# Four of a layer's seven products taken as three fp32r passes, on high and low parts made by GpSimd

## The chip, the cores and the metric

The kernel runs on one core of one Trainium2 chip. The metric is the device time of one execution, in microseconds, lower is better. The engines are named as the profile names them: PE is TensorE (PEld its weight loads), DVE is VectorE, ACT is ScalarE, POOL or Pool is GpSimd, SP is SyncE, which issues most DMAs.

## What is computed

The reference is a recommender tower: 39 embeddings of 16 numbers are gathered for each of 512 samples, pass through three layers of a compressed interaction network, and go with 16 context features through a small dense net. Cut to what matters:

```python
e = jnp.stack([tbl_f[ids[:, f]] for f in range(39)], axis=1)         # 512 x 39 x 16
def _cin_layer(X0, Xi, W, b):                                         # H = 128 outputs
    Wr = W.reshape(H, X0.shape[1], Xi.shape[1])
    return jnp.einsum('hjk,bjd,bkd->bhd', Wr, X0, Xi) + b[None, :, None]
Xi, res = e, []
for W, b in ((W0, b0), (W1, b1), (W2, b2)):
    Xi = _cin_layer(e, Xi, W, b)
    res.append(Xi.sum(axis=2))
h = jnp.concatenate([jnp.concatenate(res, axis=1), dense_ctx], axis=1)
h = relu(h @ W_top1 + b_top1); h = relu(h @ W_top2 + b_top2); y = h @ W_top3
```

Everything is float32.

## The kernel before, in words

**Tiling.** The 512 samples are 16 groups of 32. A group is 4 tiles of 128 columns (8 samples by 16 dims), so a group's operands are 512 columns wide. The kernel is a software pipeline with one period for each group. Every engine has a program of its own, written out by hand, and the engines meet at semaphores. From period 1 on, PE, DVE, Pool and SP run it in hardware loops of two periods.

**Second layer.** In period g, PE takes 10 banks for each of the 4 tiles (`layer1_bank`, L979 to L997). A bank is 512 columns (the tenth 384), in three passes at reduced input precision (fp32r): high by high, low weights by high, high weights by low. ACT multiplies seven of the ten banks by the field values (L634), DVE the other three (L795, L800), DVE adds all of them up (L816) and folds the sums (L822). The banks live in rings, 4 for ACT's and 2 for DVE's, and PE may refill one only when DVE has added its contents.

**First layer.** It is done one group ahead: during period g, PE makes the first layer of group g+1 in seven products c = 0 to 6 (`layer0`, L950), each of `w0t[:, c]` by `pairs[:, c]`, 117 rows (78 for c = 6) by 512 columns in plain float32, accumulated in the bank `p0`. A slot (t, m) is the place behind bank m of tile t. `LAYER0_SLOTS` puts the seven products at (0,4), (0,9), (1,4), (1,8), (2,4), (2,9) and (3,4). The last one releases `l0_done`; ACT then takes the high part of `p0` (L617) and DVE the low part (L771), which are the next period's operands.

**Pairs.** `pairs[:, c]` is the product of the field values `x0r` with a shifted copy of them. ACT copies `x0r` out of PSUM at slot (2,7) (L577, `copy_fields`, which also waits until all pairs of the group before are made), SP writes it to DRAM (L331) and reads it back shifted (L344): the first half (c = 0 to 3) at once, the second half after `l0_done`. Pool multiplies in place (`pair_chunk`, L479): c = 0 to 3 of group g+2 at the end of period g, c = 4 to 6 of group g+1 in tile 0 of period g.

**Pool's other work** stands in the same program order (L488 to L505): in each tile the block-diagonal operand of `gram_product` (`spread`, L474, which waits for a gram product of PE), and the ten gathers of the embeddings of group g+3 (L427), two in tile 0, four in tile 1, four in tile 2. ACT takes the gathered rows at slot (0,2) of the next period (`dims_outside`, L584).

## Time and profile before

| | us |
|---|---|
| median of 3 runs | 681.0 (680.91 to 682.17) |
| the profiled execution, its own time | 682.09 |
| its span, first to last instruction | 680.3 |
| PE busy | 646.9 (95%) |
| DVE busy | 572.9 (84%) |
| ACT busy | 561.3 (83%) |
| POOL busy | 359.6 (53%) |
| mean granted clock of PE | 0.995 |

A timeline row gives the start, the duration, the engine, the line of the kernel, the operation with output and inputs, and in brackets how long the engine stood idle before it and what ended that. Matmuls overlap, so what one takes is the distance to the next start, not its duration. Of Pool's rows, too, distances are used.

### The profile page before, as it was taken

The numbers are of one execution on the slowest core, as the hardware profiler recorded it, in microseconds if no ns is written. First come the engines' busy times: TensorE is split into PE (matmuls) and PEld (weight loads), VectorE is DVE, ScalarE is ACT, GpSimd is POOL, SyncE is SP. The second block draws the span as 40 slices with busy tenths as digits, with TensorE's granted clock in tenths as the row PEclk, the third lists the DMA queues.
The fourth block names the chain that finished last, engine by engine and source line by source line (L and its number), as shares of the span: only waits on it lengthen the run. The fifth ranks groups of instructions, "written<-read, shape, count | busy, mean of one in ns | idle before, by whom it ended". The sixth has DMA issues, their size and how long they took to land.

```text
span 680.3 us, 11318 instructions
## 1 busy us (share of the span) xinstructions
PE 646.9 (95%) x2662; PEld 483.9 (71%) x2662; DVE 572.9 (84%) x894; ACT 561.3 (83%) x1941; POOL 359.6 (53%) x394
## 2 busy tenths in 40 slices
PE   2789989999999999999999999999999999989898
PEld 2656767777777777777777777777777777767584
DVE  2548878989898998989898989898989899999870
ACT  2339879989898989988888989898989888899762
POOL 7554884664747474838384756557474323142700
PEclk9898999999999999999999999999999999999999
DMA  8215631405051414141322314050504040200000
GB/s 285 22 16 117 157 48 25 97 13 109 10 112 10 109 13 106 17 99 23 78 44 54 69 32 91 14 105 9 113 8 111 8 106 3 84 1 1 1 1 0
DMA packets 67522, 39.52 MB, mean 58 GB/s; under 512 B 58790, under 2 KB 61862, under 8 KB 65348
## 3 DMA queue, kind: packets, MB, share of 16 engines
q1 hardware_dynamic: 60463, 37.71, 24.9%
q0 software_dynamic: 5120, 1.29, 2.2%
q10 hardware_dynamic: 1904, 0.15, 0.2%
q14 instruction: 25, 0.20, 0.1%
q8 instruction: 10, 0.16, 0.1%
HBM read 32.80 MB, written 2.40 MB: 52 GB/s over the span
## 4 chain that ended last, share of the span: by engine, by line
PE 79%; DVE 9%; ACT 5%; issue 5%; DMA 1%; another core or an unknown queue 1%; DVEq 0%; ACTq 0%; SPq 0%
PE yb L992 18%; PE yb L996 17%; PE yb L993 17%; PE p L958 12%; PE pq L969 5%; DVE acc L816 3%; ACT yb L634 3%; DVE x L822 2%; PE yb L910 2%; DVE yb L800 1%; DVE x1l L874 1%; PE yb L1099 1%; PE pq L923 1%; DMA gram<-in_L_rec_W_dram 1%; PE p L1071 1%
## 5 line engine op out<-in xcount | busy, mean ns | idle before, releaser
L634 ACT ACTIVATE yb<-yb,x0t 128x128 f32<-128x128 f32 x1728 | 467.1, 366 | 58.3 <-PE yb L996 52.1
L816 DVE TENSOR_TENSOR acc<-acc,yb 128x512 f32<-128x512 f32 (+1 forms) x512 | 323.5, 668 | 34.8 <-ACT yb L634 33.8
L992 PE MATMUL yb<-w1h,x1h 128*128 128x512 f32 (+1 forms) x640 | 309.0, 483 | 8.9 <-DVE acc L816 7.6
L996 PE MATMUL yb<-w1h,x1l 128*128 128x512 f32 (+1 forms) x640 | 248.1, 388 | 0.0
L993 PE MATMUL yb<-w1l,x1h 128*128 128x512 f32 (+1 forms) x640 | 247.7, 387 | 0.0
L427 POOL DMA_INDIRECT emb<-in_table_dram,idx x160 | 152.8, 955 | 48.6 <-issue 40.5
L485 POOL TENSOR_TENSOR late<-late,x0r 117x512 f32<-117x512 f32 (+1 forms) x105 | 132.6, 1296 | 82.1 <-DMA late<-x_scratch 81.8
L992 PEld LDWEIGHTS yb<-w1h,x1h 128*128 128x128 f32 x640 | 120.6, 188 | 65.9 <-DVE acc L816 28.0
L993 PEld LDWEIGHTS yb<-w1l,x1h 128*128 128x128 f32 x640 | 121.0, 189 | 45.9 <-issue 24.8
L996 PEld LDWEIGHTS yb<-w1h,x1l 128*128 128x128 f32 x640 | 120.5, 188 | 25.2 <-DVE x1l L771 0.4
L474 POOL TENSOR_TENSOR bdiag<-mask,x0t 128x312 f32<-128x312 f32 x64 | 45.5, 711 | 145.2 <-PE pq L969 142.0
L958 PE MATMUL p<-late,w0t 117*128 117x512 f32 (+1 forms) x224 | 114.5, 592 | 0.0
L795 DVE TENSOR_TENSOR acc<-yb,x0t 128x512 f32<-128x512 f32 x128 | 87.8, 686 | 23.4 <-PE yb L996 22.0
L822 DVE TENSOR_REDUCE x<-acc 128x128 f32<-128x1152 f32 x64 | 86.0, 1344 | 0.1
L958 PEld LDWEIGHTS p<-late,w0t 117*128 117x128 f32 (+1 forms) x224 | 41.5, 189 | 7.6 <-issue 0.7
L969 PE MATMUL pq<-bdiag,x 128*128 128x320 f32 x128 | 45.0, 432 | 0.6 <-DVE x L822 0.6
L800 DVE TENSOR_TENSOR yb<-yb,x0t 128x512 f32<-128x512 f32 x64 | 44.1, 690 | 0.0
L621 ACT ACTIVATE gram<-pq 128x320 f32<-128x320 f32 x64 | 29.3, 458 | 1.2 <-PE pq L969 1.2
L969 PEld LDWEIGHTS pq<-bdiag,x 128*128 128x128 f32 x128 | 23.9, 188 | 6.2 <-DVE x L822 1.3
L617 ACT ACTIVATE x1h<-p,b0c 128x512 fp32r<-128x512 f32 x16 | 11.3, 706 | 6.1 <-PE p L958 6.1
L874 DVE TENSOR_TENSOR x1l<-gram,x1h 128x512 fp32r<-128x512 f32 x16 | 14.6, 935 | 2.0 <-ACT x1h L713 2.0
L766 DVE TENSOR_TENSOR w1l<-yb,w1h 128x512 fp32r<-128x512 f32 (+1 forms) x10 | 6.4, 673 | 10.0 <-ACT w1h L571 7.2
(108 smaller groups left out, 325.0 us busy)
## 6 DMA issues: line engine op xcount, KB each, us to landing
late<-x_scratch SPq DMA_DIRECT2D x45, 312.0 KB
late<-x_scratch SPq DMA_DIRECT2D x30, 234.0 KB
emb<-in_table_dram,idx POOLq DMA_INDIRECT x160
gram<-in_L_rec_W_dram SPq DMA_DIRECT2D x1, 2496.0 KB
x_scratch<-x0r SPq DMA_DIRECT2D x15, 156.0 KB
late<-x_scratch SPq DMA_DIRECT2D x15, 156.0 KB
w2t<-in_L_rec_W_dram SPq DMA_DIRECT2D x1, 1280.0 KB
x0t<-embt SPq DMA_DIRECT2D x64, 20.0 KB
```

The source lines that it names most:

```text
L427: pool.indirect_dma_start(emb[u][0:n, i, :], None, table[:, :], bass.IndirectOffsetOnAxis(idx[u][0:n, i:i + 1], 0)).then_inc(gathered[u], 16)
L485: pool.tensor_tensor(pairs[0:rows, c, :], pairs[0:rows, c, :], x0r[0:rows, :], ALU.mult).then_inc(pairs_ready, 1)
L634: op = act.activation(part, part, ACT.Copy, scale=x0t[u][:, t, j:j + 1])
L795: dve.tensor_tensor(acc[t % 2][:, :, at:at + BANK_F], parts(y, BANK_F), x0t[u][:, t, None, BANK_F * m:BANK_F * (m + 1)].to_broadcast([P, H ...
L800: dve.tensor_tensor(y, y, x0t[u][:, t, BANK_F * m:BANK_F * (m + 1), None].to_broadcast([P, BANK_F, HID]), ALU.mult).then_inc(dve_scaled, 1)
L816: dve.tensor_tensor(part, part, parts(y_bank(t, m), n), ALU.add).then_inc(summed, 1)
L822: dve.tensor_reduce(x2[t % 2][:, :], acc[t % 2][:, :, :], AX.X, ALU.add).then_inc(x2_ready, 1)
L958: op = pe.matmul(p0[:, :], w0t[0:rows, c, :], pairs[0:rows, c, :], start=(c == 0), stop=(c == CHUNKS - 1))
L969: pe.matmul(pq[:, 0:TILE_B * GRAM], x2[p][:, :], bdiag[p][:, :, :].rearrange("p b c -> p (b c)"), start=True, stop=True).then_inc(gram_don ...
L992: pe.matmul(y[:, 0:w], hi, w1h[:, at:at + w], start=True, stop=False)
L993: pe.matmul(y[:, 0:w], hi, w1l[:, at:at + w], start=False, stop=False)
L996: pe.matmul(y[:, 0:w], lo, w1h[:, at:at + w], start=False, stop=True).then_inc(bank_ready, 1)
```

## The change

For the groups from 2 on, the products c = 3, 4, 5 and 6 (`HALVED`) are no longer one float32 matmul but three fp32r passes. Pool makes, for each of these, the high part of the pair product (a second multiplication, written as fp32r), the product itself in place as before, and then the low part as product minus high part, behind a wait for its own two results. High and low parts live in three pairs of buffers taken in turn (`HALF_RING`), so c = 6 takes the pair of c = 3. For that, c = 3 waits for `l0_done` of the group before, and c = 6 for PE's c = 3 of the same group (`half_used`). The four weights are split once, by Pool, before its first pairs. PE waits for `pair_low` where it waited for `pairs_ready`.

```diff
+HALVED = (3, 4, 5, 6)
+HALF_RING = 3
...
+        pair_h, pair_l = spare[0:HALF_RING], spare[HALF_RING:2 * HALF_RING]
+        w0h, w0l = (spare[i][0:ROWS, 0:len(HALVED) * HID] for i in (6, 7))
...
@@ pair_chunk(g, c), Pool
+                if c not in HALVED or not at_least(g, 2):
+                    pool.tensor_tensor(pairs[0:rows, c, :], pairs[0:rows, c, :], x0r[0:rows, :],
+                                       ALU.mult).then_inc(pairs_ready, 1)
+                    return
+                k = HALVED.index(c)
+                r = k % HALF_RING
+                if c < EARLY:
+                    pool.wait_ge(l0_done, g)
+                if k >= HALF_RING:
+                    pool.wait_ge(half_used, (g - 2) * (len(HALVED) - HALF_RING) + k - HALF_RING + 1)
+                pool.tensor_tensor(pair_h[r][0:rows, :], pairs[0:rows, c, :], x0r[0:rows, :],
+                                   ALU.mult).then_inc(pair_high, 1)
                 pool.tensor_tensor(pairs[0:rows, c, :], pairs[0:rows, c, :], x0r[0:rows, :],
                                    ALU.mult).then_inc(pairs_ready, 1)
+                pool.wait_ge(pair_high, (g - 2) * len(HALVED) + k + 1)
+                pool.wait_ge(pairs_ready, g * CHUNKS + c + 1)
+                pool.tensor_tensor(pair_l[r][0:rows, :], pairs[0:rows, c, :], pair_h[r][0:rows, :].bitcast(F32),
+                                   ALU.subtract).then_inc(pair_low, 1)
...
@@ Pool, before pair_chunk(1, 0)
+            pool.wait_ge(w_hi, W0_BANKS)
+            for rows, c0, c1 in ((ROWS, HALVED[0], CHUNKS - 1), (LAST_ROWS, CHUNKS - 1, CHUNKS)):
+                of = w0t[0:rows, c0:c1, :].rearrange("p c h -> p (c h)")
+                w = slice((c0 - HALVED[0]) * HID, (c1 - HALVED[0]) * HID)
+                pool.tensor_copy(w0h[0:rows, w], of).then_inc(w0_split, 1)
+                pool.wait_ge(w0_split, 1 if rows == ROWS else 3)
+                pool.tensor_tensor(w0l[0:rows, w], of, w0h[0:rows, w].bitcast(F32), ALU.subtract).then_inc(w0_split, 1)
...
@@ layer0(g, c), PE
+                if c in HALVED and at_least(g, 2):
+                    k = HALVED.index(c)
+                    r = k % HALF_RING
+                    w = slice(k * HID, (k + 1) * HID)
+                    pe.wait_ge(pair_low, (g - 2) * len(HALVED) + k + 1)
+                    pe.matmul(p0[:, :], w0h[0:rows, w], pair_h[r][0:rows, :], start=False, stop=False)
+                    pe.matmul(p0[:, :], w0l[0:rows, w], pair_h[r][0:rows, :], start=False, stop=False)
+                    op = pe.matmul(p0[:, :], w0h[0:rows, w], pair_l[r][0:rows, :], start=False, stop=(c == CHUNKS - 1))
+                    if c == CHUNKS - 1:
+                        op.then_inc(l0_done, 1)
+                    elif k < len(HALVED) - HALF_RING:
+                        op.then_inc(half_used, 1)
+                    return
```

On Pool, in tile 0 of a period in the loop (`emb` are the gathers, `late` holds the pairs, `spare` the parts; ISA and REGISTER_ALU rows prepare a wait's value). Before:

```order
L474 TENSOR_TENSOR bdiag<-mask,x0t 128x8x39
L427 DMA emb<-in_table_dram,idx 128x16 x2
L484 REGISTER_ALU
L485 TENSOR_TENSOR late<-late,x0r 117x512 x2
L485 TENSOR_TENSOR late<-late,x0r 78x512
L474 TENSOR_TENSOR bdiag<-mask,x0t 128x8x39
```

And now, from the same operation on, as far as the second of the three products:

```order
L484 TENSOR_TENSOR bdiag<-mask,x0t 128x8x39
L437 DMA emb<-in_table_dram,idx 128x16 x2
L494 REGISTER_ALU
L505 TENSOR_TENSOR spare<-late,x0r 117x512
L507 TENSOR_TENSOR late<-late,x0r 117x512
L509 ISA
L510 ISA
L511 TENSOR_TENSOR spare<-late,spare 117x512
L505 TENSOR_TENSOR spare<-late,x0r 117x512
L507 TENSOR_TENSOR late<-late,x0r 117x512
```

Three Pool operations between the gathers of tile 0 and the `bdiag` of tile 1 have become nine; the eight gathers behind them have moved back with that `bdiag`.

On Pool at the end of a period, behind the last `bdiag`, before:

```order
L474 TENSOR_TENSOR bdiag<-mask,x0t 128x8x39
L484 REGISTER_ALU
L485 TENSOR_TENSOR late<-late,x0r 117x512 x4
L417 ISA
L417 TENSOR_TENSOR idx<-ids_all,base 128x9
```

And now:

```order
L484 TENSOR_TENSOR bdiag<-mask,x0t 128x8x39
L494 REGISTER_ALU
L496 TENSOR_TENSOR late<-late,x0r 117x512 x3
L505 TENSOR_TENSOR spare<-late,x0r 117x512
L507 TENSOR_TENSOR late<-late,x0r 117x512
L510 ISA
L511 TENSOR_TENSOR spare<-late,spare 117x512
L427 ISA
```

The fourth product has become three operations, and the next group's indices come behind them.

On PE at slot (1,8) of period 1, before (the 384 columns are bank 9 of the tile):

```order
L992 MATMUL yb<-w1h,x1h 128x512
L993 MATMUL yb<-w1l,x1h 128x512
L996 MATMUL yb<-w1h,x1l 128x512
L958 MATMUL p<-late,w0t 128x512
L992 MATMUL yb<-w1h,x1h 128x384
```

And now:

```order
L1038 MATMUL yb<-w1h,x1h 128x512
L1039 MATMUL yb<-w1l,x1h 128x512
L1042 MATMUL yb<-w1h,x1l 128x512
L995 MATMUL p<-spare 128x512
L996 MATMUL p<-spare 128x512
L997 MATMUL p<-spare 128x512
L1038 MATMUL yb<-w1h,x1h 128x384
```

One float32 matmul has become three fp32r ones in the same place; no bank of the second layer has moved.

## Rows read from the trace of the kernel before

**Rows 1.** The page: busy time by engine, and the chain's shares by line.

```profile
PE 646.9 (95%) x2662; PEld 483.9 (71%) x2662; DVE 572.9 (84%) x894; ACT 561.3 (83%) x1941; POOL 359.6 (53%) x394
...
PE yb L992 18%; PE yb L996 17%; PE yb L993 17%; PE p L958 12%; PE pq L969 5%; DVE acc L816 3%; ACT yb L634 3%; DVE x L822 2%; PE yb L910 2%; DVE yb L800 1%; DVE x1l L874 1%; PE yb L1099 1%; PE pq L923 1%; DMA gram<-in_L_rec_W_dram 1%; PE p L1071 1%
```

**Rows 2.** Timeline of PE in tile 0 of a loop period (start, us, operation).

```profile
304.72 0.40 PE L996 MATMUL yb<-w1h,x1l 128*128 128x512 f32 x1
305.33 0.50 PE L992 MATMUL yb<-w1h,x1h 128*128 128x512 f32 x1 [0.22 <-DVE acc L816]
...
308.50 0.40 PE L996 MATMUL yb<-w1h,x1l 128*128 128x512 f32 x1
308.73 1.02 PE L958 MATMUL p<-late,w0t 117*128 117x512 f32 x2
...
309.83 0.40 PE L993 MATMUL yb<-w1l,x1h 128*128 128x512 f32 x1
```

**Rows 3.** The chain that ended last, in order of time, around slot (3,4).

```profile
300.05 0.25 PE yb L996
...
300.59 0.86 ACT yb L634 x3
301.47 0.64 DVE acc L816
...
302.75 0.71 DVE x L822
...
305.33 0.50 PE yb L992
```

**Rows 4.** Timeline of PE: the last pass of five tiles in a row.

```profile
295.12 0.34 PE L996 MATMUL yb<-w1h,x1l 128*128 128x384 f32 x1
...
304.07 0.34 PE L996 MATMUL yb<-w1h,x1l 128*128 128x384 f32 x1
...
312.68 0.34 PE L996 MATMUL yb<-w1h,x1l 128*128 128x384 f32 x1
...
322.52 0.34 PE L996 MATMUL yb<-w1h,x1l 128*128 128x384 f32 x1
...
331.14 0.34 PE L996 MATMUL yb<-w1h,x1l 128*128 128x384 f32 x1
```

**Rows 5.** Timeline of POOL: a gather, the ends of period 0, a loop period.

```profile
30.48 0.92 POOL L427 DMA_INDIRECT emb<-in_table_dram,idx  x1 [0.30 <-issue]
...
60.21 5.03 POOL L485 TENSOR_TENSOR late<-late,x0r 117x512 f32<-117x512 f32 x4 [12.73 <-DMA late<-x_scratch]
...
83.71 0.73 POOL L474 TENSOR_TENSOR bdiag<-mask,x0t 128x312 f32<-128x312 f32 x1
...
305.22 5.04 POOL L485 TENSOR_TENSOR late<-late,x0r 117x512 f32<-117x512 f32 x4 [4.84 <-DMA late<-x_scratch]
...
310.84 0.71 POOL L474 TENSOR_TENSOR bdiag<-mask,x0t 128x312 f32<-128x312 f32 x1 [0.27 <-POOL idx L421]
```

**Rows 6.** Timeline of ACT: the embedding copies (L584) and a copy of `x0r`.

```profile
35.14 0.47 ACT L584 ACTIVATE embq<-emb 128x160 f32<-128x160 f32 x1
...
90.55 0.47 ACT L584 ACTIVATE embq<-emb 128x160 f32<-128x160 f32 x1 [2.42 <-DMA emb<-in_table_dram,idx]
...
295.28 0.62 ACT L577 ACTIVATE x0r<-pq 117x512 f32<-117x512 f32 x1
...
308.40 0.55 ACT L584 ACTIVATE embq<-emb 128x160 f32<-128x160 f32 x1
```

**Rows 7.** Timeline of SP's queue: issue of the second half's reads.

```profile
301.18 1.12 SPq L344 DMA_DIRECT2D late<-x_scratch  x3
```

**Rows 8.** Stretches: busy time and count by engine, PE clock, DMA share, GB/s.

```profile
307.00:308.00 1.00, 1.00 (x6) 0.75 (x4) 1.00 (x3) 1.00 (x5) 1.00 (x2) 1.00 0.07 12
```

**Rows 9.** Two lines of DVE: duration in ns, min/median/max, first and last start.

```profile
L816 DVE TENSOR_TENSOR acc<-acc,yb x512: 547/679/703, 51.2 to 628.7; 128x512 f32<-128x512 f32 x150, 128x384 f32<-128x384 f32 x21
...
L874 DVE TENSOR_TENSOR x1l<-gram,x1h x16: 677/692/1760, 632.7 to 657.3; 128x512 fp32r<-128x512 f32 x16
```

More of the change, by code:

```diff
@@ L251, in tower @@
         bias_ready = sem("bias_ready")
+        w0_split = sem("w0_split")
+        pair_high = sem("pair_high")
+        pair_low = sem("pair_low")
+        half_used = sem("half_used")
         h1_done = sem("h1_done")
@@ L1040, in _ @@
             period(0, 0, 2)
+            pe.wait_ge(w0_split, 4)
             period(1, 1, 2)
```

## The prediction

> **What bounds the kernel now.** I read the page first. PE is busy 95% of the span, DVE 84%, ACT 83%, Pool 53%; the chain that ended last runs on PE for most of its length, and the lines of the second layer (L992, L993, L996) have 52% of it [rows 1]. So a column taken off PE is worth time, as long as it lies on the chain. The first layer's line L958 has 12% of it: 0.12 x 680 = 82 us. There are 16 x 7 = 112 such products, the trace counts two records for each.
>
> What one costs is read from starts, since matmuls overlap. L958 starts at 308.73; the next bank's second pass starts at 309.83, and one pass before it takes about 0.23 (308.50 to 308.73), so the product held PE for 1.10 - 0.23 = 0.87 us [rows 2]. The ends of tiles say the same: the tile that ends at 322.52 held three products and took 9.84, the one that ends at 304.07 held two and took 8.95 [rows 4], a difference of 0.89. But 82 us is 95 products of 0.87, not 112: about one in seven is not on the chain. The chain in order of time shows which. Behind bank 4 of tile 3 (pass at 300.05) it leaves PE for ACT (300.59), goes through DVE's sum (301.47) and fold (302.75), and comes back to PE only with the second bank of the next period, at 305.33 [rows 3]. Slot (3,4), with c = 6, lies inside this stretch. PE finishes its own work there at 304.72 + 0.23 = 304.95 and then waits 0.38 for DVE [rows 2].
>
> I call S the start of a period: 304.07 plus 0.17 for a pass of 384 columns, 304.25 [rows 4]. From 268.05, the same place one period earlier by four tiles of 9.84, 8.62, 8.95 and 8.61, a period is 36.02.
>
> **PE's side of the change.** Each halved product is three passes of 0.23, 0.69 together, for one of 0.88, the mean of both readings: 0.19 less. Bounds: 0.17 if each pass costs the 0.24 that some passes behind a float32 product do, against 0.89; 0.21 if the three take 0.68. In each of the 14 periods that make groups 2 to 15 there are four. c = 3, 4 and 5 lie on the chain, 3 x 0.19 = 0.57. c = 6 lies beside the stretch over ACT and DVE, which starts with bank 4, ahead of it, and is not shortened; PE then waits 0.38 + 0.19 = 0.57 there instead of 0.38. It counts zero, its cover is the chain of [rows 3], and without that it would be worth 14 x 0.19 = 2.7 us. Sum: 14 x 0.57 = 8.0 us (7.1 to 8.8). The period becomes 36.02 - 0.57 = 35.45. DVE and ACT do the same work as before, in step with PE, and idle less.
>
> **Pool's side.** This is what the change costs. One pair operation is 1.25 us: four take 5.04 by their record, which overlaps the next by some 0.05 [rows 5]. Each halved product adds two: 8 x 1.25 = 10.0 us a period. The low part also waits for Pool's own last result. No such pair exists before; the nearest row is the `bdiag` that waited 0.27 for Pool's own index operation [rows 5]. I take 0.25 for each of the four, 1.0 us; the bounds are zero (the wait is hidden) and 0.54 each (two semaphores, each at that price), 0 to 2.2 us.
>
> What Pool had to do before: in period 0 it ran without a stall from 60.21 to the end of the `bdiag` at 83.71 + 0.73, pairs, gathers and all, 24.2 us [rows 5]; in the loop the wait of 0.27 comes on top, 24.4. So Pool's loop becomes 24.4 + 10.0 + 1.0 = **35.4 us, against a period of 35.45**. It has idled a third of the time and will idle none; this is the number that decides the case. It lies between 34.4 and 36.6.
>
> Where does Pool stand in the period? It begins the next group's pairs when the shifted fields have landed, at 305.22, S + 0.97 [rows 5]. That landing hangs on ACT's copy of `x0r` at 295.28 [rows 6], ahead of c = 5 and c = 6; these are 0.38 shorter now, 0.19 of it is given back in PE's wait behind S. So the landing will be at S + 1.35, and I call Pool's start P. Then:
> - c = 0 is ready at P + 1.3 = S + 2.7. PE wants it at 308.73, S + 4.5 [rows 2], and 0.2 later now: 2.0 us of room.
> - c = 6 is ready before the last eight gathers and three `bdiag`: 35.4 - 8 x 1.25 - 3 x 0.75 = P + 23, S + 24.5; PE wants it at 300.1, S + 32. ACT's next copy of `x0r`, which waits for these pairs too, is at S + 27. c = 3 to 5 have more room, and so have the two buffer waits: `l0_done` is past by then, and c = 3 has left PE ahead of tile 1's last pass, 322.52, S + 18.3 [rows 4], when Pool comes to c = 6 at S + 20.5. With two pairs in flight and one to spare, the ring does not bind.
> - The last gather ends 0.7 before the loop's end, P + 34.7, S + 36.05, which is 0.6 behind the next S. ACT wants the rows at 308.40, S + 4.15 [rows 6], now 4.35: 3.75 us to land.
>
> With 35.4 against 35.45 nothing drifts. With Pool's loop at 36.6 it would drift 1.15 each in the 11 loop periods with gathers, use up the room of 2.0 and cost 10.6 us. For the middle, where the loop is a few tenths over, I take off 0.5 us. In period 0 Pool's order is the old one but for c = 3; and the last two periods have no gathers, so Pool has room in these. The split of the weights is four operations at 47 us, where Pool idled 12.73 us before its first pairs [rows 5]: free.
>
> **Sum.** 8.0 - 0.5 = 7.5 us. The profiled execution took 682.09, 1.1 over the median of the three runs, so it becomes 674.6, and the median 681.0 - 7.5 = **673.5**.
>
> **Do Pool and DVE disturb each other?** Behind the last period, where DVE subtracts with both inputs in SBUF (L874), its operation takes up to 1760 ns beside Pool's, 677 alone. In the loop, Pool's pair products run beside DVE's sums, which read one input from PSUM, and of 512 sums none took over 703 ns [rows 9]. The Trainium skill ("SBUF — State Buffer", section "SBUF: two separate sides") has GpSimd share a port pair with VectorE, an exclusive lock held for an instruction, taken by VectorE operations with two SBUF inputs or in a 2-port mode. By it the loop's sums take no lock, and the trace agrees; read as a rule for every VectorE operation, it would speak against giving Pool 112 more. I price that as a rival: eight operations that each hold DVE by 1760 - 677 = 1.1 us are 8.7 us a period, far over DVE's idle share of 16%.
>
> **The rivals.**
> - *Pool's loop is the bound.* For: 35.4 against 35.45 leaves nothing, and its own waits are priced from a single kind of row. Against: two microseconds of room absorb a drift of 0.18 in each of 11 periods. With a loop of 35.7 to 36.1, 0.8 to 5 us are lost: 675 to 679, and 679 to 682 up to 36.4. Chance 18%, of which 3 land within 0.2% of no change.
> - *The gathers land late and ACT stalls, so the kernel is slower.* Place: ACT's `dims_outside` at slot (0,2), a wait in the middle of its scalings. For: the last gathers now go out together with the second half of the shifted reads, which are issued at 301.18 [rows 7]. In period 0 that was already so: the last gather ended at 83.7, ACT got the rows at 90.55, 6.85 us later, and had waited 2.42 [rows 5, 6]. Against: small context loads were in the queues as well there; in a quiet place the gather that ended at 31.40 was used at 35.14 [rows 5, 6], at most 3.74 us; and in the loop the transfers have drained by 307, S + 2.8 [rows 8], before ACT's slot. Price: with landing in 6.85 ACT waits 3.1 less what the period grows; if 0.8 of that reaches PE, the period grows by 1.4 to 36.85, 0.8 over before, so 11 x 0.8 - 3 x 0.57 = 7 us slower, 688. With landing in 5.5 it is 683. It decides from about 5.0 us of landing time, where the period is back at 36.02. Chance 12%, 3 of it within 0.2%. The Trainium skill ("DMA: Bandwidth & Descriptors", section "Anatomy of one DMA — SWDGE (gpsimd) path") gives about 2.0 us as the fixed cost of such a DMA. By that figure ACT would not wait at all; no row here shows a landing by itself, only that it took at most 3.74 in the quiet.
> - *c = 6 counts too*, because the stretch over ACT and DVE shortens once its waits for PE move: 14 x 0.76 = 10.6 us, 670.5. Against: its start, bank 4, lies ahead of c = 6. Chance 9%.
> - *Pool holds DVE*, as priced above: 14 x (8.7 less 5 of idle time) = 50 us slower. Chance 1%, by [rows 9].
>
> **How the numbers follow.** The forecast, 671.5 to 675.5, has 60%; the rivals have 18, 12, 9 and 1. The range leaves out the gather stall, the lock and the far end of Pool's bound, and takes in c = 6: 670 to 679. About 0.2%, 1.4 us, is what a measurement can tell from no change. Faster: 60 + 15 + 9 = 84%. Within 0.2%: 3 + 3 = 6%. Slower: 9 + 1 = 10%.
>
> **What would show it.** Right: periods of 35.4 to 35.5, PE's wait for DVE at the second bank of a period grown by 0.2, the three passes at 0.68 together, Pool busy around 500 us with almost no idle time from period 2 to 12, pair operations still 1.25 apart, DVE's sums still 0.68. Wrong: PE waiting at slot (0,4) for Pool, with the wait setting in after some periods (Pool's bound); ACT waiting at L584 for the gathers in each period (the stall); sums of DVE over 1 us; or no growth of PE's wait for DVE (c = 6 counts).

## The result, and the profile after

The prediction was wrong. The changed kernel takes **712.4 us** (median, 711.2 to 715.0) beside 681.0 for the kernel before on the same chip: ratio 1.047, interval 1.045 to 1.049, slower where 673.5 was forecast. Its profiled execution took 713.18 us with a span of 711.4.

First the page of the changed kernel: busy time, the chain by engine, and groups of instructions (busy us, mean ns, then the idle time ahead of them and what ended it). L1038, L1039, L1042 are what L992, L993, L996 were, L667 is L634, L849 is L816, and L828 is what L795 was.

```profile
PE 650.5 (91%) x2718; PEld 498.1 (70%) x2718; DVE 574.6 (81%) x894; ACT 559.8 (79%) x1941; POOL 503.7 (71%) x510
...
PE 75%; DVE 8%; issue 6%; ACT 6%; DMA 3%; SPq 2%; another core or an unknown queue 1%; DVEq 0%
...
L667 ACT ACTIVATE yb<-yb,x0t 128x128 f32<-128x128 f32 x1728 | 468.1, 372 | 91.7 <-PE yb L1042 87.7
...
L1038 PE MATMUL yb<-w1h,x1h 128*128 128x512 f32 (+1 forms) x640 | 291.5, 456 | 37.5 <-DVE acc L849 34.2
...
L828 DVE TENSOR_TENSOR acc<-yb,x0t 128x512 f32<-128x512 f32 x128 | 88.1, 689 | 44.6 <-PE yb L1042 42.9
```

The same two groups of the kernel before:

```profile
L634 ACT ACTIVATE yb<-yb,x0t 128x128 f32<-128x128 f32 x1728 | 467.1, 366 | 58.3 <-PE yb L996 52.1
...
L992 PE MATMUL yb<-w1h,x1h 128*128 128x512 f32 (+1 forms) x640 | 309.0, 483 | 8.9 <-DVE acc L816 7.6
```

Against [rows 1]: PE's share fell from 95% to 91%, Pool went from 359.6 to 503.7 us as forecast, and the work of DVE and ACT is what it was. Only Pool is much busier, and it is idle for 29% of the span, so the 31 us are waiting. They are not where a rival put them: DVE and ACT wait longer for PE (ACT 87.7 us, before 52.1), and PE waits longer for DVE (34.2, before 7.6).

The last passes of five tiles in a row, as in [rows 4], tell in which tiles:

```profile
278.47 0.33 PE L1042 MATMUL yb<-w1h,x1l 128*128 128x384 f32 x1
...
288.51 0.34 PE L1042 MATMUL yb<-w1h,x1l 128*128 128x384 f32 x1
...
298.19 0.34 PE L1042 MATMUL yb<-w1h,x1l 128*128 128x384 f32 x1
...
306.64 0.34 PE L1042 MATMUL yb<-w1h,x1l 128*128 128x384 f32 x1
...
316.98 0.34 PE L1042 MATMUL yb<-w1h,x1l 128*128 128x384 f32 x1
```

Tiles 0 to 3 of this period take 10.04, 9.68, 8.45 and 10.34 us. In the kernel before they took 8.61, 9.84, 8.62 and 8.95 [rows 4]. Tiles 1 and 2 are shorter by 0.16 and 0.17, what the change promised. Tiles 3 and 0 are longer by 1.4 each. Every period that has gathers is stretched in this way, most of them by as much (period 1 by less, a few by more); the mean of the 12 periods from 123.81 to 587.69 is 38.66, before it was 36.05, and 12 x 2.61 = 31.3 is the whole difference of the spans (711.4 - 680.3 = 31.1).

What happens in tile 3 is seen in the timeline of the changed kernel, all engines, from the middle of that tile (SP's row: its shifted reads, L354; its store of `x0r` had gone out at 307.45):

```profile
308.65 0.98 POOL L437 DMA_INDIRECT emb<-in_table_dram,idx  x1 [0.16 <-issue]
...
309.65 6.15 SPq L354 DMA_DIRECT2D late<-x_scratch  x6
...
310.03 0.39 PE L1042 MATMUL yb<-w1h,x1l 128*128 128x512 f32 x1
310.26 0.70 PE L1015 MATMUL pq<-bdiag,x 128*128 128x320 f32 x2
...
311.26 0.40 PE L1042 MATMUL yb<-w1h,x1l 128*128 128x512 f32 x1
...
312.43 0.92 POOL L437 DMA_INDIRECT emb<-in_table_dram,idx  x1 [0.30 <-issue]
...
313.15 0.69 DVE L828 TENSOR_TENSOR acc<-yb,x0t 128x512 f32<-128x512 f32 x1 [2.89 <-PE yb L1042]
...
313.35 0.40 PE L1042 MATMUL yb<-w1h,x1l 128*128 128x512 f32 x1
...
314.49 0.50 PE L1038 MATMUL yb<-w1h,x1h 128*128 128x512 f32 x1 [0.74 <-issue]
...
314.63 0.71 POOL L484 TENSOR_TENSOR bdiag<-mask,x0t 128x312 f32<-128x312 f32 x1 [1.28 <-remote]
...
314.63 1.11 ACT L667 ACTIVATE yb<-yb,x0t 128x128 f32<-128x128 f32 x4 [3.23 <-PE yb L1042]
...
319.64 0.63 PE L1038 MATMUL yb<-w1h,x1h 128*128 128x512 f32 x1 [1.63 <-DVE acc L849]
```

PE's records run on without a gap: bank 3 of the tile has its last pass at 310.03, the gram product follows at 310.26, bank 4 has its last pass at 311.26. But DVE, which waits for bank 3 alone, starts at 313.15, 3.12 us behind that pass; ACT, which waits for bank 4, starts at 314.63, 3.37 behind; and Pool, which waits for the gram product, starts at 314.63 as well. Then the delay comes back: PE finds its rings full, idles 0.74 at 314.49 (the profile names no releaser there; DVE's sum that frees the bank had just ended), and waits 1.63 for DVE at the second bank of the next period, where it waited 0.22 in [rows 2]. I call this the stall.

How long such a start should take is shown by the same kernel in a run on another chip (e8, below), at the same place of a period:

```profile
288.58 0.39 PE L1042 MATMUL yb<-w1h,x1l 128*128 128x512 f32 x1
...
289.01 0.69 DVE L828 TENSOR_TENSOR acc<-yb,x0t 128x512 f32<-128x512 f32 x1 [0.20 <-PE yb L1042]
...
289.82 0.40 PE L1042 MATMUL yb<-w1h,x1l 128*128 128x512 f32 x1
...
290.25 1.11 ACT L667 ACTIVATE yb<-yb,x0t 128x128 f32<-128x128 f32 x4 [0.42 <-PE yb L1042]
...
295.26 0.50 PE L1038 MATMUL yb<-w1h,x1h 128*128 128x512 f32 x1 [0.36 <-DVE acc L849]
```

It is 0.43 us from the start of the last pass, for both. So in the stall DVE and ACT start 2.7 and 2.9 us late. The trace settles what is late. Besides the rows it holds the time of each semaphore update, which no view prints. In e8 the update for each of the two banks comes 0.41 us behind the start of its last pass (288.99 and 290.23). In the changed kernel banks 3 to 6 of the tile have their last passes at 310.03, 311.26, 312.66 and 313.35, and their updates at 313.12, 314.61, 314.71 and 314.76. The last three stand 0.15 us apart in all, and PE's records give a bank at least three passes of 0.23, so PE can't have computed them one behind the other that late: **it had computed on time, and its signals were held and came together.** The updates that ACT, DVE and Pool make for their scalings, sums and `bdiag`, as far as the trace holds them, come at most 0.014 us behind the end of an instruction, in the stall too, so it is PE's that were held. In the slow kernel DVE's start for bank 3 of tile 3 is late by 1.0 to 3.9 us in each of the eleven periods 2 to 12, and by nothing in period 13.

**The runs fell into two sorts.** The kernels that went together ran on one chip. In three sets the kernel before took 681 to 682 us (I call that the 681 sort), in four 673 (the 673 sort). Two of the 673 sets and the last 681 set (e18) have the same chip number, 4, in the record, so no run shows that the sort goes with the chip. A loop period takes 36.05 in the profile of before and 36.06 in that of e1, nearly the same kernel, on the other sort. The difference comes about ahead of that: the last pass of the first tile is at 54.82 and at 48.74, the end of period 1 at 123.81 and at 115.80. PE's clock falls for a few microseconds at the start. The stretches of the kernel before (columns as in [rows 8]: the granted clock is the third number from the end):

```profile
26.00:28.00 2.00, 1.94 (x10) 1.80 (x11) 2.00 (x5) 1.07 (x3) 1.39 (x3) 0.59 0.10 10
28.00:30.00 2.00, 2.00 (x12) 2.00 (x12) 2.00 (x5) 0.00 (x0) 1.70 (x2) 0.55 0.40 55
```

and of e1, on the 673 sort:

```profile
26.00:28.00 2.00, 2.00 (x18) 2.00 (x17) 1.74 (x3) 0.57 (x1) 1.47 (x2) 0.89 0.38 50
28.00:30.00 2.00, 1.76 (x17) 1.56 (x14) 0.01 (x1) 1.26 (x4) 1.28 (x3) 1.00 0.11 8
```

That is not what sets the sorts apart: e1 passes through such a fall as well, 2 to 4 us earlier (granted 0.76, 0.50 and 0.89 in the three stretches from 22 to 28 us; 0.50 is the 1.2 GHz level). In both PE had stood idle just ahead of it, for 2.07 and 2.87 us. One thing does tell them apart in every trace: on the 681 sort update records are missing, also in the kernel before (574 for PE's 640 banks, and 564 to 601 in the others), while on the 673 sort there are 636 to 641. The result above is of the 681 sort. Part of the start's difference is the stall itself, of which more below. What the two sorts differ in, and whether it is the chip or what stands around it, no run tells.

### The profile page after: what moved, and what is told of

The parts are those of the page before. It is cut to its first block, busy times and chain, and to the rows that moved or that the text cites. A ratio compares the mean times of both kernels' runs of the same rounds, so it can differ in the third digit from the quotient of the medians.

```text
span 711.4 us, 11614 instructions
## 1 busy us (share of the span) xinstructions
PE 650.5 (91%) x2718; PEld 498.1 (70%) x2718; DVE 574.6 (81%) x894; ACT 559.8 (79%) x1941; POOL 503.7 (71%) x510
## 4 chain that ended last, share of the span: by engine, by line
PE 75%; DVE 8%; issue 6%; ACT 6%; DMA 3%; SPq 2%; another core or an unknown queue 1%; DVEq 0%
PE yb L1042 18%; PE yb L1038 17%; PE yb L1039 17%; PE p L1004 5%; PE pq L1015 5%; ACT yb L667 4%; DVE acc L849 3%; DVE x L855 2%; PE p L996 2%; PE p L997 2%; PE p L995 2%; DMA gram<-in_L_rec_W_dram 2%; PE yb L943 1%; DVE yb L833 1%; DVE x1l L907 1%
## 5 line engine op out<-in xcount | busy, mean ns | idle before, releaser
L667 ACT ACTIVATE yb<-yb,x0t 128x128 f32<-128x128 f32 x1728 | 468.1, 372 | 91.7 <-PE yb L1042 87.7
L849 DVE TENSOR_TENSOR acc<-acc,yb 128x512 f32<-128x512 f32 (+1 forms) x512 | 324.7, 671 | 43.0 <-ACT yb L667 39.1
L1038 PE MATMUL yb<-w1h,x1h 128*128 128x512 f32 (+1 forms) x640 | 291.5, 456 | 37.5 <-DVE acc L849 34.2
L1039 PE MATMUL yb<-w1l,x1h 128*128 128x512 f32 (+1 forms) x640 | 250.7, 392 | 0.0
L1042 PE MATMUL yb<-w1h,x1l 128*128 128x512 f32 (+1 forms) x640 | 250.4, 391 | 0.0
L1038 PEld LDWEIGHTS yb<-w1h,x1h 128*128 128x128 f32 x640 | 122.0, 191 | 90.9 <-DVE acc L849 53.3
L1039 PEld LDWEIGHTS yb<-w1l,x1h 128*128 128x128 f32 x640 | 122.6, 192 | 35.2 <-issue 11.5
L1042 PEld LDWEIGHTS yb<-w1h,x1l 128*128 128x128 f32 x640 | 122.2, 191 | 25.8 <-issue 0.4
L828 DVE TENSOR_TENSOR acc<-yb,x0t 128x512 f32<-128x512 f32 x128 | 88.1, 689 | 44.6 <-PE yb L1042 42.9
L505 POOL TENSOR_TENSOR spare<-late,x0r 117x512 fp32r<-117x512 f32 (+1 forms) x56 | 72.5, 1295 | 9.1 <-PE p L997 8.8
L511 POOL TENSOR_TENSOR spare<-late,spare 117x512 fp32r<-117x512 f32 (+1 forms) x56 | 72.1, 1288 | 4.9
L1004 PE MATMUL p<-late,w0t 117*128 117x512 f32 (+1 forms) x112 | 57.4, 593 | 0.0
L1004 PEld LDWEIGHTS p<-late,w0t 117*128 117x128 f32 (+1 forms) x112 | 20.4, 189 | 4.2 <-issue 1.1
```

The costliest lines, as they stand in the source:

```text
L505: pool.tensor_tensor(pair_h[r][0:rows, :], pairs[0:rows, c, :], x0r[0:rows, :], ALU.mult).then_inc(pair_high, 1)
L667: op = act.activation(part, part, ACT.Copy, scale=x0t[u][:, t, j:j + 1])
L828: dve.tensor_tensor(acc[t % 2][:, :, at:at + BANK_F], parts(y, BANK_F), x0t[u][:, t, None, BANK_F * m:BANK_F * (m + 1)].to_broadcast([P, H ...
L849: dve.tensor_tensor(part, part, parts(y_bank(t, m), n), ALU.add).then_inc(summed, 1)
L1004: op = pe.matmul(p0[:, :], w0t[0:rows, c, :], pairs[0:rows, c, :], start=(c == 0), stop=(c == CHUNKS - 1))
L1038: pe.matmul(y[:, 0:w], hi, w1h[:, at:at + w], start=True, stop=False)
```

## The experiments

All runs, with the kernel before on the same chip (ratios of medians with their interval; e8 has one run, so no interval):

| run | what it is | sort | us | ratio |
|---|---|---|---|---|
| result | the changed kernel | 681 | 712.4 | 1.047 (1.045 to 1.049) |
| e1 | before, gathers (0,2,4,4) by tile | 673 | 673.8 | 1.001 (0.999 to 1.002) |
| e2, e10, e13 | changed, no gathers | 673 | 666.3, 665.9, 666.0 | 0.989, 0.988, 0.990 (0.985 to 0.992) |
| e3, e9, e12, e17 | changed, no passes on PE | 673 | 674.0, 674.0, 674.0, 674.2 | 1.001 to 1.002 (1.000 to 1.004) |
| e4 | passes alone, Pool as before | 673 | 666.8 | 0.990 (0.988 to 0.992) |
| e5 | the changed kernel again | 681 | 719.5 | 1.056 (1.050 to 1.063) |
| e6 | passes alone, gathers (0,2,4,4) | 681 | 675.6 | 0.991 (0.988 to 0.994) |
| e7 | changed, passes for c = 3, 4 only | 681 | 717.7 | 1.052 (1.046 to 1.058) |
| e8 | the changed kernel, third chip (one run) | 673 | 669.5 | 0.994 |
| e14 | changed, small shifted reads | 673 | 666.8 | 0.991 (0.989 to 0.992) |
| e11, e15, e16 | changed, two products halved | 673 | 669.1, 669.3, 669.3 | 0.993, 0.995, 0.994 (0.991 to 0.997) |
| e18 | two products halved (two runs) | 681 | 695.5 | 1.019 (1.004 to 1.034) |

### The change taken apart (e1 to e4)

The first theory was that late gathers beside the shifted reads make the stall. e1 is the kernel before with its gathers moved two tiles back:

```diff
-GATHERS_OF_TILE = (2, 4, 4, 0)
+GATHERS_OF_TILE = (0, 2, 4, 4)
```

> The kernel before, with the ten gathers of a period moved from 2, 4, 4, 0 in tiles 0 to 3 to 0, 2, 4, 4. Nothing else changes: the first layer stays float32, and Pool has no more work. Theory A (the gathers and the shifted reads of the fields, in flight together at the end of a period, hold PE up): the changed kernel's stall of about 2.8 us in tile 3 appears here too, tile 3 takes 10 us or more instead of 8.95, and the time rises by 15 to 30 us, to 696 to 711. Theory B (PE's three passes on parts cause it, or Pool's arithmetic): no stall, 681 to 683.

e2 leaves the gathers out:

```diff
-                            gather(1 - u, todo.pop(0))
+                            todo.pop(0)
```

> The changed kernel with the gathers of groups 3 to 15 left out (ACT takes what lies in the buffers, without a wait), all arithmetic kept. Theory A: no stall in tile 3, periods of 35.4 to 35.5 as the prediction had them, 673 to 675. Theory B: the stall stays, since the passes and Pool's operations stay; the time is 705 or more.

e3 leaves all on Pool and takes the passes from PE:

```diff
-                    pe.matmul(p0[:, :], w0h[0:rows, w], pair_h[r][0:rows, :], start=False, stop=False)
-                    pe.matmul(p0[:, :], w0l[0:rows, w], pair_h[r][0:rows, :], start=False, stop=False)
-                    op = pe.matmul(p0[:, :], w0h[0:rows, w], pair_l[r][0:rows, :], start=False, stop=(c == CHUNKS - 1))
+                    op = pe.matmul(p0[:, :], w0t[0:rows, c, :], pairs[0:rows, c, :], start=False, stop=(c == CHUNKS - 1))
```

> The changed kernel with PE taking each of the four products as one float32 matmul on the pairs again, behind the same waits; Pool still makes all the parts, which nobody reads. Theory A: the stall stays, and the time is that of the changed kernel and 8 us more, 712 to 722. Theory B in its first form (PE's passes on the parts): the stall goes and the time is 681 to 684. In its second form (Pool's arithmetic): it stays.

e4 leaves the passes on PE, on parts that Pool fills once at the start, and gives Pool back its old work:

```diff
-                if c not in HALVED or not at_least(g, 2):
+                if True:
...
+            for buf in list(pair_h) + list(pair_l):
+                pool.tensor_copy(buf[0:ROWS, :], w0t[0:ROWS, 0:4, :].rearrange("p c h -> p (c h)")).then_inc(w0_split, 1)
...
-                    pe.wait_ge(pair_low, (g - 2) * len(HALVED) + k + 1)
+                    pe.wait_ge(pairs_ready, g * CHUNKS + c + 1)
```

> The changed kernel with PE's three passes for the four products, but Pool makes only the plain pairs; the passes read parts that were filled once at the start, so the first layer of groups 2 to 15 is left out in effect. Pool's order is that of the kernel before. Theory A: no stall, and the gain of PE by itself: 3 x 0.19 x 14 = 8.0 us, ratio 0.988 (10.6 us, 0.984, if c = 6 counts). Theory B in its first form: the stall is here, 705 or more.

Measured: 1.001, 0.989, 1.001 and 0.990, none with a stall. As it turned out the set was of the 673 sort, so they say nothing of the stall, which the changed kernel does not have there either; they price the parts. In e4 the last passes of five tiles are

```profile
256.67 0.34 PE L1044 MATMUL yb<-w1h,x1l 128*128 128x384 f32 x1
...
265.44 0.34 PE L1044 MATMUL yb<-w1h,x1l 128*128 128x384 f32 x1
...
275.11 0.34 PE L1044 MATMUL yb<-w1h,x1l 128*128 128x384 f32 x1
...
283.57 0.34 PE L1044 MATMUL yb<-w1h,x1l 128*128 128x384 f32 x1
...
292.23 0.34 PE L1044 MATMUL yb<-w1h,x1l 128*128 128x384 f32 x1
```

tiles of 8.77, 9.67, 8.46 and 8.66, a period of 35.56 against the 36.02 of the kernel before. That is PE's part of the change: 0.46 in a period, 6.3 us in all (673.06 - 666.75). Pool's part without PE's (e3) costs 0.9 us.

### The changed kernel again, and two reductions (e5 to e7)

e5 is the changed kernel. e6 is e4 with the gathers of e1. e7 is the changed kernel with c = 5 and 6 taken by PE as one float32 product, while Pool works in full:

```diff
+                    if c > 4:
+                        op = pe.matmul(p0[:, :], w0t[0:rows, c, :], pairs[0:rows, c, :], start=False, stop=(c == CHUNKS - 1))
+                        if c == CHUNKS - 1:
+                            op.then_inc(l0_done, 1)
+                        return
```

> The changed kernel once more, beside the others on this chip. All theories: a ratio near the first measurement, 1.047, with the stall in tile 3 of each loop period.

> PE's passes on parts filled once (Pool makes plain pairs only; the first layer of groups 2 to 15 is left out in effect), and the gathers late, 0, 2, 4, 4 by tile. So the passes meet gathers and shifted reads in flight, but Pool has none of the new arithmetic. Theory C (the passes and the gathers in flight together are enough): a stall in tile 3 and a ratio over 1.02. Theory D (Pool's new operations are needed as well, since the passes wait for parts that Pool has just written): no stall, ratio 0.99 as without the late gathers.

> The changed kernel with PE taking three passes for c = 3 and 4 only, and one float32 matmul on the pairs for c = 5 and 6, behind the same waits; Pool unchanged. If what counts is that passes run in tile 3 beside the shifted reads, the stall goes: ratio 0.99 to 0.995 (two of three gains left). If it is the product before (c = 3, 4), or something that the passes leave behind, the stall stays: over 1.02.

Measured: 1.056, 0.991, 1.052; the set was of the 681 sort. The stall is repeatable (e5), and it stands in e7 at its full size, so the passes of c = 5 and c = 6, which lie next to it, are not needed for it. DVE in e7, for a bank whose last pass starts at 274.55:

```profile
278.82 0.69 DVE L828 TENSOR_TENSOR acc<-yb,x0t 128x512 f32<-128x512 f32 x1 [3.14 <-PE yb L1047]
```

is 3.8 us late. In e6 the tiles are those of e4 (tile 1 is up to 0.4 longer in a few periods), and DVE starts in tile 3 as it should. This is the run that excludes the simplest cause. In e6, too, gathers and shifted reads are in flight together in tile 3. The second half of tile 3, by stretch, in the changed kernel (the last two columns are the DMA share and GB/s):

```profile
311.64:316.98 5.34, 4.24 (x19) 2.87 (x17) 3.09 (x5) 2.35 (x8) 2.11 (x3) 1.00 0.82 187
```

and in e6:

```profile
331.30:335.70 4.40, 4.40 (x22) 3.61 (x21) 3.90 (x6) 3.98 (x15) 3.53 (x4) 1.00 0.84 199
```

The DMA engines are as busy in e6, 0.84 at 199 GB/s, and PE has no idle time. So load on the DMA engines does not make the stall. The changed kernel itself has a period that says what is needed: period 13, which stores and reads as all others but gathers nothing, since there is no group 16. Its tile 3 takes 8.66 (last passes at 579.03 and 587.69), with the DMA engines at 0.86, and DVE starts its bank 3 on time:

```profile
582.84 0.69 DVE L828 TENSOR_TENSOR acc<-yb,x0t 128x512 f32<-128x512 f32 x1 [0.20 <-PE yb L1042]
```

In e5 that tile takes 8.66 as well, and in e7 8.95, with c = 5 and c = 6 as float32 products; both start on time. As far as one period of each of three runs can show it, the stall needs the gathers, and it needs something that e6's gathers don't bring.

### The third chip, and the chain of causes that was left (e8 to e17)

> The changed kernel, once more beside the next three, since the first four runs were on another chip (its kernel before took 673) than the changed kernel (681). If the stall belongs to the kernel on every chip, ratio 1.04 to 1.06; if it belongs to a chip, it may be absent.

> PE takes one float32 matmul on the pairs for each of the four products, Pool still makes all parts: the run e3 again, beside the changed kernel. If PE's passes are part of the cause: no stall, ratio 1.00. If gathers and shifted reads in flight beside Pool's arithmetic are the cause and the first run was on a chip where they do not collide: the stall is here, ratio over 1.04.

> The gathers of groups 3 to 15 left out: the run e2 again, beside the changed kernel. If the gathers are part of the cause: no stall, ratio 0.99. If the chip was the difference: ratio over 1.04.

e11 halves two products in place of four, c = 3 and 4 (the weights' split shortened to match):

```diff
-HALVED = (3, 4, 5, 6)
+HALVED = (3, 4)
```

> Only c = 3 and 4 are halved. Pool's loop is 24.4 + 4 x 1.25 + 0.5 = 29.9 us, so the last gather ends at S + 30.6, about where the shifted reads begin, not among them. If the overlap of gathers with the reads beside a full Pool is the cause: no stall or a small one, ratio 0.990 to 0.995. If the passes as such are: ratio over 1.03.

Here the changed kernel took 669.5 beside 673.3, in a single run: 0.6% **faster** (the ten runs of the kernel before lie between 672.7 and 674.1), without a stall, and e9 and e10 repeated e3 and e2. The same program is 5% slower on one sort and faster on the other; that was the finding of this set. e11 is as fast as the kernel with four, at half of Pool's new work.

The next two sets were meant for the 681 sort, and fell on the 673 sort. e12 and e17 are e3, e13 is e2, e15 and e16 are e11. e14 cuts the shifted reads of groups 2 to 15 to 64 of 512 columns, so that the first layer is not computed:

```diff
+                        w = 64 if at_least(g, 2) else GROUP_N
-                        src = bass.AP(first.tensor, first.offset, [[row, FIELDS], [row, n], [1, GROUP_N]])
+                        src = bass.AP(first.tensor, first.offset, [[row, FIELDS], [row, n], [1, w]])
```

> The changed kernel with one edit: PE takes c = 3 to 6 as one float32 product of the pairs, as the kernel before, while Pool still makes high parts, products and low parts, and PE waits for them. Meant for a chip on which the kernel before takes 681 us. Theory (the stall in tile 3 is brought about by transfers beside a Pool that has no idle time; PE's passes play no part): tile 3 at 9.8 us or more in the loop, ratio 1.03 to 1.06. Rival (PE's three passes in a row are what the stall needs): tile 3 at 8.6, ratio 1.000 to 1.004, as on the two chips where the kernel before takes 673. If the kernel before takes 673 on this chip, ratio 1.00 by both and nothing is told apart.

> The changed kernel without the gathers of groups 3 to 15 (ACT works on old rows); Pool's arithmetic and the shifted reads as in the changed kernel. Theory (the gathers in flight beside the shifted reads delay PE's signals): no stall, tile 3 at 8.6 to 8.7, period 35.5 to 35.6, ratio 0.987 to 0.992. Rival (Pool's arithmetic alone does it): tile 3 at 9.8 or more, ratio above 1.02.

> The changed kernel with the shifted reads cut to 64 of 512 columns for groups 2 to 15 (the rest of the pairs is what was there before, so the first layer isn't computed); the number of reads and all waits are kept. Theory (it needs gathers and shifted reads in flight together): tile 3 at 8.5 to 9.0, ratio 0.985 to 1.00. Rival (the gathers alone do it, or the number of packets rather than their bytes): tile 3 at 9.8 or more, ratio 1.03 to 1.06.

> The changed kernel with HALVED = (3, 4): c = 5 and c = 6 are made and multiplied as in the kernel before. Pool has four arithmetic operations less in a period, 5.3 us, and the last eight gathers go out 5.3 us earlier, at about S + 31 in place of S + 36. Theory (the stall is the gathers of tile 2 in flight beside the shifted reads, which comes of Pool being late): no stall or a small one, ratio 0.992 to 1.00, as 0.9934 on the third chip. Rival (any halved product on Pool brings the stall on): ratio 1.03 to 1.06.

> The kernel of e15 (HALVED = (3, 4)) once more, in the hope of a chip on which the kernel before takes 681 us. There: if the stall comes of Pool being late (the last gathers in flight beside the shifted reads), tile 3 at 8.6 to 9.0 us and ratio 0.985 to 1.00; if any halved product on Pool brings it on, tile 3 at 9.8 or more and ratio 1.03 to 1.06. On a chip where the kernel before takes 673, ratio 0.992 to 0.997 by both.

> The kernel of e12 once more (no passes on PE, Pool's work in full). On a chip where the kernel before takes 681: if Pool's work with the transfers is enough for the stall, tile 3 at 9.8 or more and ratio 1.03 to 1.06; if PE's three passes are needed, tile 3 at 8.6 and ratio 1.000 to 1.004. On a chip where it takes 673, ratio 1.00 by both.

On the stall they are inconclusive. They bear on another thing: the 2.7 us by which the changed kernel is behind e4 on the 673 sort (669.5 and 666.75). Part of it is the second rival of the prediction in small. Timeline of ACT in e8, in tile 0:

```profile
300.09 0.50 ACT L617 ACTIVATE embq<-emb 128x160 f32<-128x160 f32 x1 [1.62 <-DMA emb<-in_table_dram,idx]
```

Groups of instructions of e8 and then of e14, the copy of the gathered rows:

```profile
L617 ACT ACTIVATE embq<-emb 128x160 f32<-128x160 f32 x16 | 8.1, 508 | 13.5 <-DMA emb<-in_table_dram,idx 13.5
```

```profile
L618 ACT ACTIVATE embq<-emb 128x160 f32<-128x160 f32 x16 | 8.6, 536 | 1.7 <-DMA emb<-in_table_dram,idx 1.7
```

ACT waits 13.5 us for gathered rows in e8, 1.7 with the reads cut down (666.8 us, all of e4's gain), and 2.6 with two products halved, where Pool issues the gathers earlier. By itself that does not show that the reads slow the gathers: in e14 Pool waits less for the reads, too, and its last gather ends 2.2 us ahead of the period's end, in e8 0.2 to 0.8 behind it. The update records show it. In e1 the six gathers of tiles 1 and 2 have landed 1.3 to 2.3 us after the end of their issue, the four of tile 3, beside the reads, 3.8 to 5.6 us after it; in e14 all ten, the last four beside the cut reads, have landed after 1.3 to 2.3 us. (These are the loop periods of one of the two buffers, whose records are complete.) So the gathers land late beside the shifted reads.

What it costs is less than the 2.7 us. From the end of period 1 to that of period 13 e8 takes 428.21 and e4 426.94, and e8's longer tiles are those behind ACT's longer waits (tile 1 at 10.10 in place of 9.67 behind the wait of 1.62 above). So some 1.3 us come of ACT's waits. The other 1.5 lie ahead of the end of period 1, where the profiles of this sort differ by 2.4 among themselves (113.50 in e13, 115.85 in e8, but also 115.80 in e1, which has none of Pool's new work); no run tells their cause.

### Two halved products where the stall lives (e18)

> The kernel with HALVED = (3, 4) a third time, in the hope of a chip on which the kernel before takes 681 us. There, if the stall comes of Pool being late, tile 3 at 8.6 to 9.0 us and ratio 0.985 to 1.00; if any halved product on Pool brings it on, tile 3 at 9.8 or more and ratio 1.03 to 1.06. On a chip where it takes 673, ratio 0.992 to 0.997 by both.

The last run fell on the 681 sort: 1.019, from two runs of 691.1 and 699.9. Neither expectation holds as written. Tile 3 is back at 8.96 in most periods, but tile 0 takes 9.5 to 10.1 in place of 8.6. The late signals now come earlier: in the changed kernel bank 0 of tile 3 is on time in all periods but one, here it is late in each from period 2 on (in e5 and e7 in most). DVE, for a bank whose last pass starts at 299.43:

```profile
302.48 0.69 DVE L828 TENSOR_TENSOR acc<-yb,x0t 128x512 f32<-128x512 f32 x1 [1.70 <-PE yb L1042]
```

2.6 us late. The stall has moved forward with the gathers and become smaller. Pool has 14% less work here (432 us) than in the changed kernel and waits 84 us for the shifted reads, so a Pool without idle time is not needed either.

**What is known of the stall, and what stays open.** On the 681 sort it came in three kernels (the changed one, e7, e18), in the periods with gathers, where gathers are issued one behind the other for 10 us (eight, with one `bdiag` between: 303.02 to 313.35 above, 1.25 apart). It did not come in the loop of the kernel before and of e6, where a wait for the gram product parts the eight into fours some 4 to 5 us apart, nor in a period without gathers. During it Pool does nothing but gathers and `bdiag`, so Pool's arithmetic beside PE is not it; it only decides when the gathers go.

The update records tie the stall to the row more closely. In each of these periods (1 to 12, in e18 2 to 12) three to five of PE's held updates come together, 0.05 to 0.11 us apart, and the first of them 1.1 to 1.4 us after the last gather's issue ends: at 314.61 above (313.35 and 1.26), and in e18 at 302.46 (301.37 and 1.09). The row moved forward by some 3.5 us in e18, and the burst with it. The shifted reads are not needed. In period 4 of e18 the last two banks of tile 2 and the first two of tile 3 have their last passes at 222.73, 223.32, 224.82 and 225.50, and PE's updates come at 226.51, 226.56, 226.63 and 226.68. ACT has waited for the first of them, and all that is over before the reads are issued:

```profile
224.37 0.92 POOL L437 DMA_INDIRECT emb<-in_table_dram,idx  x1 [0.31 <-issue]
...
225.29 0.33 SPq L341 DMA_DIRECT2D x_scratch<-x0r  x1
...
226.53 3.70 ACT L667 ACTIVATE yb<-yb,x0t 128x128 f32<-128x128 f32 x14 [1.26 <-PE yb L1042]
...
227.34 1.13 SPq L354 DMA_DIRECT2D late<-x_scratch  x3
```

The kernel before has the stall as well, once, before its loop, behind a row of ten gathers (35.28 to 47.48):

```profile
46.56 0.92 POOL L427 DMA_INDIRECT emb<-in_table_dram,idx  x1 [0.31 <-issue]
...
47.95 0.39 PE L996 MATMUL yb<-w1h,x1l 128*128 128x512 f32 x1
...
49.65 0.69 DVE L795 TENSOR_TENSOR acc<-yb,x0t 128x512 f32<-128x512 f32 x1 [2.99 <-PE yb L996]
```

Five banks of the first tile have their last passes 0.68 apart, from 46.58 to 49.31, and their updates come at 49.53, 49.58, 49.63, 49.68 and 49.73, the first 2.05 behind the last gather's issue. DVE starts bank 3 at 49.65, 1.3 us late. All profiles of the 681 sort have such a burst near 50 us, and none of the 673 sort: in e1, behind a row of ten at 31.46 to 43.67, each update comes 0.41 behind its pass, those within 2 us of the row's end (43.78, 44.47 and 45.16) too. So a part of the difference at the start is this stall.

A row of gathers one behind the other is thus what all stalled stretches have in common, but it is not enough. In period 1 of e18 the eight stand in as close a row (103.06 to 113.58), there is no burst, and DVE starts bank 3 of tile 3 on time (117.11, its last pass 116.68). And on the 673 sort the same row does no harm. No run varied the row alone. What is shown is that PE's signals are held, not its work, and that they are let go as the row of gathers ends; by what path gathers hold them is open. The Trainium skill ("Perfetto Trace Analysis", section "Tensor Engine Instruction (MATMUL, LD_WEIGHTS)") says that the end of a matmul's record is estimated from its size, and that the write's acknowledgement and the semaphore's update come behind it and are not in the profile. The trace agrees as far as PE's rows go, which showed nothing of the 2.7 us; the updates stand in the trace as records of their own.

## Why the prediction was wrong, point by point

- **The step that failed** is the one that takes no term of its own: that "DVE and ACT do the same work as before, in step with PE, and idle less". Every term was a duration of work or a wait for something late. That PE's signals could reach DVE, ACT and Pool up to 4 us late was in no row that the prediction read, though the trace of the kernel before has it once, at its start (above). In the result they were held while eight gathers went out in a row, and DVE and ACT did not stay in step: it costs 2 x 1.4 us a period, and tiles 1 and 2 win back 0.33. No rival had it; the slower one named ACT's wait for the gathers, 12%, and ACT waits nothing for gathers in e5 or e7.
- **Four products at 0.19.** On both sorts tiles 1 and 2 became 0.16 and 0.17 shorter. The three passes take 0.69 as forecast (in e8 L995 starts at 285.38, the next bank at 286.07); the float32 product was 0.86, less than either reading. Tile 3, with two of them, lost 0.30. The term is 0.46 in a period and 6.3 us in place of 8.0: mis-sized, just below its lower bound of 7.1.
- **c = 6 counts zero.** Right: tile 0 of e4 is 0.16 longer than before, and PE's pause at the second bank of a period went from 0.61 between starts (304.72 and 305.33 in [rows 2]) to 0.75 (294.51 and 295.26 in e8).
- **Pool's loop, 35.4.** Right in kind, somewhat too dear. In e8, Pool's rows of one pair product:

```profile
275.34 1.29 POOL L505 TENSOR_TENSOR spare<-late,x0r 117x512 fp32r<-117x512 f32 x1
276.59 1.30 POOL L507 TENSOR_TENSOR late<-late,x0r 117x512 f32<-117x512 f32 x1
277.97 1.30 POOL L511 TENSOR_TENSOR spare<-late,spare 117x512 fp32r<-117x512 f32 x1
279.24 1.28 POOL L505 TENSOR_TENSOR spare<-late,x0r 78x512 fp32r<-78x512 f32 x1
```

  are 1.25, 1.38 and 1.27 apart, so Pool's own wait costs 0.13, not 0.25. From its first product at 260.13 to the end of the last `bdiag` at 295.03 it works 34.9, and then waits 1.33 for the reads. Its bound was not reached, so 0.5 us for it was too much.
- **The gathers** are the term that was mis-sized the other way. In e8 the last one ends at 294.30 and ACT has the rows at 300.09, 5.8 us later (4.3 to 5.8 in periods 2 to 12); the forecast gave 3.75 of room and took that to be enough, by a landing "in a quiet place". Its rival named 5.0 us as the turning point, and its price was too high, since it let most of ACT's wait reach PE. By the 2.0 us that the Trainium skill gives ("DMA: Bandwidth & Descriptors", section "Anatomy of one DMA — SWDGE (gpsimd) path") ACT would not have waited. The trace agrees for a gather without reads in flight (in e1 mostly 1.3 to 1.5 us after the end of an issue of 0.95), and not beside the reads (3.8 to 5.6).
- **The ring does not bind.** Wrong in a small way: Pool waits for PE's c = 3 ahead of c = 6 in four of the changed kernel's periods, 8.8 us together, and in eleven of e5's. In e8 it is one wait of 0.4. Pool then waits for the shifted reads at the end of the same period, so nothing shows that these waits cost time.
- **Pool holds DVE.** Rightly put aside: DVE's sums take 671 ns in the mean.
- On the 673 sort the sum comes out as 6.3 - 2.5 = 3.8 us faster, half of the 7.5 forecast. Of the 2.5 some 1.3 are traced to the gathers. The time is inside the range by its ratio (0.994 x 681 = 677), but with both terms off: 6.3 for 8.0, and 2.5 for 0.5. On the 681 sort it is 31 slower.

In three periods of the changed kernel the stall costs more, 11.59 for tile 0 (and in a fourth tile 3 takes 12.40). The stretch behind it is at a granted clock of 0.57, most of it at the 1.2 GHz level, behind one in which PE had worked 1.03 of 2.62 us:

```profile
316.98:319.60 2.62, 1.03 (x5) 0.55 (x4) 2.62 (x5) 2.62 (x12) 2.36 (x2) 1.00 0.56 141
319.60:323.60 4.00, 3.96 (x10) 3.12 (x11) 3.46 (x7) 3.19 (x13) 3.92 (x5) 0.57 0.09 12
```

## What to carry to other kernels

Giving an idle engine work also moves everything that stands behind that work in its program. Here eight gathers moved from a place with pauses into one row; price the moved DMAs, in more than one set of runs, before the arithmetic. A kernel that is faster in one set and 5% slower in another is no gain: none of the complete versions here is faster than the kernel before on both sorts, and half of the change (two halved products) gives all of the gain on the one and less than half of the loss on the other. Where consumers wait for an engine whose records show no gap, measure from its record to their start: that distance, 0.43 us here, is a quantity like any other. Updates that come closer together than the work behind them can be done tell late signals from late work.

## What the runs showed of the hardware

- PE's semaphore updates can be held for 1 to 4 us and then come in threes to fives, 0.05 to 0.11 us apart, while its records run on at 0.23 us a pass; in each stalled period of the loop such a burst comes 1.1 to 1.4 us after the last gather's issue ends (2.05 us at the start of the kernel before).
- The same kernel takes 673 us in some sets and 681 in others, by its start, and another one 669.5 and 712 to 719.
- A gather issued while shifted reads are in flight landed 3.8 to 5.6 us after the end of its issue (e1), without them 1.3 to 2.3.
- A Pool operation that waits for Pool's own two last results costs 0.13 us.
